# Experts' borders packed into two integers, and the result copy moved to the end of its pass

## What is computed

```python
h_shared = _swiglu(flat @ shared_in_w.T)
out_shared = h_shared @ shared_out_w.T + shared_out_b
...
e_probs = jax.nn.softmax(e_sel, axis=-1)
topv, topi = jax.lax.top_k(e_probs, K)
...
h_expert = _swiglu(flat @ expert_in_w.T)
...
for e in range(E):
    routed = routed + comb[:, e:e + 1] * (h_expert @ expert_out_weight[e].T)
return (out_shared + routed).reshape(Bx, Tx, Cx)
```

## Time and profile before

| what | value |
|---|---|
| median of 3 runs | 781.32 us (780.72 to 784.39) |
| profiled execution, its own time | 779.41 us |
| its span | 777.6 us |
| PE busy | 734.0 us (94%) |
| DVE busy | 409.9 us (53%) |
| ACT busy | 262.7 us (34%) |
| POOL busy | 168.0 us (22%) |
| PE's first instruction of the experts' loop part (L1611) | 563.5 us |
| last turning in the loop (L1611) | 711.7 us |

### The profile page before, as it was taken

One profiled execution on the slowest core, in us unless ns is written; L12 is line 12 of the kernel. 1 busy time (PEld: TensorE's weight loads), 2 busy tenths in 40 slices (PEclk: granted clock), 3 DMA queues, 4 the chain that ended last, 5 costly groups with the idle time before them and its releaser, 6 DMA issues.

```text
span 777.6 us, 11923 instructions
## 1 busy us (share of the span) xinstructions
PE 734.0 (94%) x4217; PEld 456.4 (59%) x4217; DVE 409.9 (53%) x809; ACT 262.7 (34%) x387; POOL 168.0 (22%) x167
## 2 busy tenths in 40 slices
PE   4998999998799999999999999999889999999998
PEld 4664777775457755656575654445745555555554
DVE  4877987795457766696435442222146434421154
ACT  2761222222255223236534213333345524422000
POOL 3320000000006000002222224444612222211462
PEclk9999999999999999999999999999969999999999
DMA  9200002000004114001234320111367866333674
GB/s 239 91 1 0 1 2 79 31 1 1 13 2 135 55 62 156 1 0 27 54 98 145 107 54 17 46 48 55 109 211 247 324 234 231 122 122 125 191 206 133
DMA packets 24368, 73.37 MB, mean 94 GB/s; under 512 B 7138, under 2 KB 7484, under 8 KB 20225
## 3 DMA queue, kind: packets, MB, share of 16 engines
q1 hardware_dynamic: 8607, 39.74, 15.3%
q0 software_dynamic: 10624, 24.99, 11.1%
q10 hardware_dynamic: 5090, 8.01, 2.8%
HBM read 57.38 MB, written 15.31 MB: 93 GB/s over the span
## 4 chain that ended last, share of the span: by engine, by line
PE 77%; DVE 9%; ACT 7%; DMA 3%; issue 2%; ACTq 1%; POOL 0%; DVEq 0%; POOLq 0%
PE banks L1272 58%; PE banks L1314 6%; PE banks L1302 6%; PE banks L1611 2%; DMA y_rows<-xT 1%; ACT W L411 1%; PE banks L1327 1%; DMA big<-in_proj_mat 1%; DVE st L733 1%; PE banks L1295 1%; DVE W L710 1%; PE banks L1482 1%; DVE xn L1092 1%; ACT big L579 1%; ACTq L457 1%
## 5 line engine op out<-in xcount | busy, mean ns | idle before, releaser
L1272 PE MATMUL banks<-W,xT 128*125 128x512 f16 (+1 forms) x1392 | 319.9, 384 | 8.0 <-ACT xT L677 1.9
L1272 PEld LDWEIGHTS banks<-W,xT 128*125 128x125 f16 (+1 forms) x1392 | 166.0, 122 | 139.0 <-issue 17.6
L1272 PE MATMUL banks<-xT,W 128*128 128x500 f16 (+1 forms) x720 | 131.3, 344 | 1.8 <-DVE xn L1224 1.4
L1272 PEld LDWEIGHTS banks<-xT,W 128*128 128x128 f16 x720 | 70.7, 98 | 60.4 <-issue 4.4
L710 DVE SCALAR_TENSOR_TENSOR W<-stg,W 128x2048 f16<-128x2048 f32 x30 | 68.8, 2313 | 42.7 <-ACT W L411 42.7
L1272 PE MATMUL banks<-W,big 128*125 128x512 f16 x360 | 81.5, 380 | 0.0
L1242 DVE CAST xT<-banks 128x1024 f32 x23 | 28.1, 1222 | 73.4 <-PE banks L1611 73.4
L1272 PEld LDWEIGHTS banks<-W,big 128*125 128x125 f16 x360 | 48.3, 136 | 29.2 <-issue 2.3
L353 POOL DMA_INDIRECT xn<-h_rows,tokidx x28 | 35.1, 1253 | 125.8 <-PE banks L1611 119.6
L342 POOL TENSOR_TENSOR big<-xn,big 125x512 f16<-125x512 f32 x20 | 23.5, 1173 | 173.1 <-ACT big L594 173.1
L411 ACT ACTIVATE W<-stg 128x2048 f16<-128x2048 f32 x30 | 56.4, 1904 | 0.0
(11 more groups left out here) (292 smaller groups left out, 861.3 us busy)
## 6 DMA issues: line engine op xcount, KB each, us to landing
stg<-in_units SPq DMA_DIRECT2D x30, 1024.0 KB, 5.0
y_rows<-xT ACTq DMA_DIRECT2D x29, 256.0 KB
h_rows<-big POOLq DMA_DIRECT2D x10, 500.0 KB, 3.6
out_x<-x SPq DMA_DIRECT2D x10, 224.0 KB
stg<-in_wqkT SPq DMA_DIRECT2D x2, 1024.0 KB, 11.5
x<-in_x SPq DMA_DIRECT2D x2, 896.0 KB
x<-in_x SPq DMA_DIRECT2D x1, 448.0 KB
xn<-h_rows,tokidx POOLq DMA_INDIRECT x28, 5.2
```

The lines of the kernel that those rows point to most:

```text
L1272: ins = te.matmul(dst, lhs(sl, c), rhs(sr, c), start=(first and c == 0 and k == 0), stop=(last and c == n - 1 and k == 2))
```

## The change

1. The eight ends of the experts are packed four by four, to the base 28, into two integers. DVE computes them in three instructions (one addition, two multiply-adds) where it wrote nine integers in two. `etab` holds two integers.
2. Each engine loads two integers in place of eight (`borders`). Division and remainder on registers are put where a border is used: at the end of each pass and between the experts' loops.
3. ACT and DVE read them during the shared product, behind group 21 of 24. PE reads them where it did.
4. On ACT, `result(0)` stands right behind the first high copy, ahead of the units U_EXP + 4 and + 5; a pass is `high(i + 1)`, `result(i + 1)`, and `result(total)` behind the loop goes. With that the units behind an expert follow the result copy of its last pass.

```diff
+PACK = NT + 1
...
-        etab = sb("etab", [1, EXP + 1], I32)
+        etab = sb("etab", [1, 2], I32)
+        etabf = sb("etabf", [1, 6])
...
+        def borders(eng):
+
+            ends = []
+            for z in range(2):
+                four = eng.value_load(etab[0:1, z:z + 1], min_val=0, max_val=PACK ** 4 - 1)
+                for k in range(4):
+                    e = 4 * z + k
+                    ends.append(eng.snap((four // PACK ** k) % PACK, min_val=e + 1, max_val=NT - EXP + e + 1))
+            return ends
...
@@ ACT @@
                         unit(U_EXP + n // 4 - 1)
-
-
-            act.wait_ge(S["etab_rdy"], 1)
-            starts = [act.value_load(etab[0:1, e:e + 1], min_val=e, max_val=NT - EXP + e) for e in range(1, EXP + 1)]
-            ends, total = starts, starts[EXP - 1]
+                    if n == 21:
+                        act.wait_ge(S["etab_rdy"], 1)
+                        starts = borders(act)
+                        ends, total = starts, starts[EXP - 1]
...
             s.activation(hgT[:, 0, 0], turned[0], ACT.Copy).then_inc(S["hg_h"], 1)
+            result(0)
             unit(U_EXP + 4)
             unit(U_EXP + 5)
             for e in range(EXP):
                 with act.Fori(0 if e == 0 else starts[e - 1], ends[e]) as i:
-                    result(i)
                     high(i + 1)
+                    result(i + 1)
                 for u in late_units(e):
                     unit(u)
-            result(total)
...
@@ DVE, route @@
-                v.tensor_copy(etab[0:1, 0:EXP], nt8[0:1, 1, :])
-                v.tensor_tensor(etab[0:1, EXP:EXP + 1], nt8[0:1, 1, EXP - 1:EXP], nt8[0:1, 0, EXP - 1:EXP], ALU.add).then_inc(S["etab_rdy"], 1)
+                ends8 = seen[0:1, TILES, :]
+                link(v.tensor_tensor(ends8, nt8[0:1, 1, :], nt8[0:1, 0, :], ALU.add))
...
+                v.scalar_tensor_tensor(out=etab[:, :], in0=quads[:, :, 1], scalar=float(PACK * PACK), in1=quads[:, :, 0],
+                                       op0=ALU.mult, op1=ALU.add).then_inc(S["etab_rdy"], 1)
...
@@ DVE, shared product; the same at n == 21 @@
+                    if n == 21:
+                        dve.wait_ge(S["etab_rdy"], 1)
+                        starts = borders(dve)
...
@@ PE, ahead of the loop @@
-            starts = [pe.value_load(etab[0:1, e:e + 1], min_val=e, max_val=NT - EXP + e) for e in range(1, EXP + 1)]
+            starts = borders(pe)
```

More of the change, by code:

```diff
@@ L1190, in route @@
                     link(v.tensor_tensor(nt8[:, 1, e:e + 1], nt8[:, 1, e - 1:e], nt8[:, 0, e - 1:e], ALU.add))
-                v.tensor_copy(etab[0:1, 0:EXP], nt8[0:1, 1, :])
-                v.tensor_tensor(etab[0:1, EXP:EXP + 1], nt8[0:1, 1, EXP - 1:EXP], nt8[0:1, 0, EXP - 1:EXP], ALU.add).then_inc(S["etab_rdy"], 1)
+                ends8 = seen[0:1, TILES, :]
+                link(v.tensor_tensor(ends8, nt8[0:1, 1, :], nt8[0:1, 0, :], ALU.add))
+                pairs = ends8.rearrange("p (z a b) -> p z a b", z=2, a=2)
+                link(v.scalar_tensor_tensor(out=etabf[:, 0:4].rearrange("p (z a) -> p z a", z=2), in0=pairs[:, :, :, 1], scalar=float(PACK), in1=pairs[:, :, :, 0],
+                                            op0=ALU.mult, op1=ALU.add))
+                quads = etabf[:, 0:4].rearrange("p (z a) -> p z a", z=2)
+                v.scalar_tensor_tensor(out=etab[:, :], in0=quads[:, :, 1], scalar=float(PACK * PACK), in1=quads[:, :, 0],
+                                       op0=ALU.mult, op1=ALU.add).then_inc(S["etab_rdy"], 1)
                 dve.wait_ge(S["etab_rdy"], 1)
@@ L1229, in _ @@
                         unit(U_EXP + n // 4 - 1)
-            dve.wait_ge(S["etab_rdy"], 1)
-            starts = [dve.value_load(etab[0:1, e:e + 1], min_val=e, max_val=NT - EXP + e) for e in range(1, EXP + 1)]
-            ends, total = starts, starts[EXP - 1]
+                    if n == 21:
+                        dve.wait_ge(S["etab_rdy"], 1)
+                        starts = borders(dve)
+                        ends, total = starts, starts[EXP - 1]
             dve.wait_ge(S["turned"], 1)
```

## The result

| | before | after |
|---|---|---|
| median | 782.86 us (780.72 to 784.67, 4 runs) | 813.13 us (809.85 to 814.99, 4 runs) |
| ratio, 95% interval | 1 | 1.0383 (1.033 to 1.0436) |
| profiled execution, its own time | 779.41 us | 814.99 us |
| its span | 777.6 us | 813.0 us |

The change makes the kernel 3.8% slower. The forecast was 808.0 us, range 795 to 817.

What follows compares the result with a forecast made beforehand. PE, busy 94% of the span, was taken as the bound. 779.41 - 3.0 (entry) + 20.4 (stalls) + 9.9 (clock) - 0.6 (given back) = 806.1 us, or 808.0 against the median; own range 802 to 813, wider 795 to 817.

Steps and rivals of the forecast that it cites:

- Rival (c): At the experts' borders: no stall, so only the entry's saving counts and the kernel is faster, 777.7 us; chance 0.07.
- The border of an expert: At six experts' ends, late weight units delay DVE's low copy, so PE stalls 3.4 us each, 20.4 us in all.
- The clock after each stall: Behind each of six border stalls PE's granted clock falls, costing 1.65 us each, 9.9 us in all.
- (a): At the six borders: the stalls come but the clock stays up, 798.1 us; chance 0.14.
- (b): Behind the six border stalls: the lower clock lasts twice as long per stall, 817.9 us; chance 0.07.
- The entry: Start of the experts' loop: fewer border loads and the first result copy ahead of the units save 3.0 us.
- L(1) doesn't spoil that: At the loop's entry: DVE's next low copy, behind the units, ends at 574.6, before the first product ends at 575.7.
- Rival (d): At the loop's entry: nothing is saved and the stalls stay, 811.0 us; its chance is inside the forecast's 0.70.
- The packing: DVE's three small instructions and unpacking on registers at pass ends: costed at nothing; other ends 0.4 and 1.2 us.
- Given back: In the loop: stalled passes leave time for waits on the previous result's DMA, returning 0.6 us, between 0 and 1.

Runs made afterwards that it cites:

- experiment 2: Two variants of the changed kernel with the low copy ahead of the units: DVE's loops shifted by one pass, 785.01 us; ACT's shifted too, 777.52 us.
- e1_pack_only: The changed kernel with ACT's old order put back, packed borders and early reads kept: 778.77 us, ratio 0.9984 to the kernel before.
- e2_order_only: The kernel before, with its eight border loads per engine, given only ACT's new order: 811.04 us, ratio 1.0397.
- e9_double_low: The changed kernel with DVE writing the low half of each of the twelve late units twice: 842.72 us, ratio 1.0776.
- e3_both_shifted: The changed kernel with ACT's and DVE's loops shifted by one pass, the second high and low copies ahead of the entry's units: 777.52 us, ratio 0.9962.
- e11_shifted_again: The same file as e3_both_shifted, run again beside the kernel before: 780.09 us, ratio 0.9987.

## Why the prediction was right, and where it was off

**Direction and mechanism: right.** The six idles ahead of a turning, ended by DVE's low copy, came as forecast. Rival (c), no stall, holds only for kernels that move L (experiment 2) or leave ACT's order (e1_pack_only).

**"The border of an expert", 6 x 3.4 = 20.4 us: 19.6 measured.** The chain held step by step. The units follow R by 1.40 us (587.93 - 586.53) where 1.36 was taken from the earlier trace rows. DVE's pair is 1.94 us behind, keeps it 4.41 us, and PE starts 0.44 us after the copy, where 0.42 was taken. The Trainium skill (Advanced Engine Details and Errata, Control Flow Timing) would have added about 0.1 us for the loop's end between R and the units. In the trace of the kernel after the compare-and-branch itself takes 40 to 50 ns on ACT (L699). The spacing of 1.40 us leaves room for 0.04 us, and the stalls came out shorter than 3.4 us rather than longer, so here the measurement speaks for less.

**"The clock after each stall", 9.9 us: 7.8 measured. This term was somewhat too large, and it left something out.** It priced a loss of clock of 1.65 us per border and took it for all that a stall costs behind its idle time; the turning behind a stall was put at its 1.06 us without a reason. Measured behind each stall are, on average, 1.30 us of clock and 1.16 us of slower turning, 14.8 us in all. The turning's part is not the clock. Stretches behind the first border, kernel after, and the turning behind the third:

```profile
594.00:597.50 3.50, 1.56 (x13) 1.20 (x13) 1.50 (x2) 0.00 (x0) 0.00 (x0) 1.00 0.96 351
598.00:601.00 3.00, 3.00 (x9) 1.05 (x9) 1.23 (x1) 1.02 (x1) 0.95 (x1) 0.50 0.84 303
601.00:604.00 3.00, 3.00 (x15) 1.42 (x14) 0.00 (x0) 0.00 (x0) 0.00 (x0) 0.98 0.32 126
...
632.26:634.46 2.20, 2.19 (x16) 1.67 (x17) 0.00 (x0) 0.00 (x0) 0.00 (x0) 0.50 1.00 398
```

The turning from 595.94 runs at 1.00 up to 597.5 at least and takes 2.17 us. Then the clock is at 0.50, its 1.2 GHz level, in M, and back near 2.4 GHz in the stretch from 601. The third turning runs at 0.50 throughout and takes 2.31 us, hardly more. The missed evidence was in the earlier trace rows: at 0.50 T(1), at 567.35, took 2.22 us behind a wait and T(0), whose addresses are constants, 1.87. T(1) took 2.20 to 2.23 us at the entry of every kernel. The prediction carried this 2.22 us over to the new entry and did not ask what it means for the turnings behind the stalls.

**Rivals (a) and (b): both fell, (b) at five borders of six.** The clock does fall, behind all six stalls (6.15 to 7.42 us for M). At the third border it was at 0.50 from 632.26 to 638.00 us, through the whole turning and most of M, which is some twice as long as at the others, and M lost 2.07 us; the mean of the six is below the forecast's 1.65. That it is paid at each wait anew agrees with the rule drawn on (the Trainium skill, TensorE: Matmul & The Clock Gate, HAM oscillation). The rows add how often: it was paid behind all eighteen border waits of 3.2 to 7.9 us (after, e2_order_only and e9_double_low), behind five of six of 1.8 us, behind three of six of 1.1 to 1.2 us, and behind none of six of 0.2 us.

**"The entry", -3.0 us: -3.3 measured, from other parts, so the close agreement is partly luck.** T(0) waits 2.08 us in place of 3.23, for POOL's announcement, as forecast: 1.15 us. M(0) no longer waits for R(0) and starts 2.98 us sooner, where 2.48 was forecast. M(0) took 5.91 us where 7.2 was expected, a larger gain from the clock. "L(1) doesn't spoil that" was wrong: L(1) ended at 578.49, only 0.08 us before M(0). T(2) had to wait 0.31 us and took 2.22 us instead of 1.06, by the same slow turning, which gave 1.5 us back. That the loads, and not T(0), held H(0) and L(0) was a reading on 0.07 us (565.41 + 0.23 against 565.71) and changes nothing in the sum. Rival (d) is out.

**"The packing", nothing: right.** DVE's three instructions took 0.15 us each and hid; e1_pack_only shows no loss from the divisions and remainders between passes. The loads, now two per queue, left the shared product alone: ACT still paused 1.28 us at each pass there.

**"Given back", 0.6 us: about 0.4 measured.**

**The sum.** Against the profiled execution 26.7 us were expected. The loop and entry made 30.7. The errors are -0.8 for the idles, -2.1 for the clock, +7.0 for the turnings, -0.3 at the entry and +0.2 for what is given back, together +4.0. The clock term, 2.1 too high, hid part of the 7.0 that was left out; that much of the agreement is luck. The median of 813.13 us lies in the range of 795 to 817, just past the upper end of the forecast's own 802 to 813. The profiled span grew by another 4.6 us, which belongs to the clock of that execution in unchanged code. The forecast stood on the median of 781.32 us, where the four runs now give 782.86, so against 26.7 us the medians moved by 30.3.

## What to carry to other kernels

When a copy that waits for a product is moved within an in-order queue, look at what stands behind it at the border of the loop as well as inside it: here weight conversions stood there, and another engine's copy behind them, so moving one instruction by one place shifted the chain by a whole product (5.35 us) against 2.0 us of slack. Price a stall of PE by its idle time plus what follows it, here the clock of the next product and a slower turning, whose register work had no time to run ahead; 3.3 us of idle cost 5.7. A change with two parts should be measured in two parts: one half of this one was harmless, and the loss was wholly in the other.

## What the runs showed of the hardware that was not expected

- A turning of 16 products of 128x128 with register addresses took 2.1 to 2.3 us when PE's queue had just waited, be it 0.17 us with a granted clock of 1.00 behind it or 7.9 us with one of 0.50, and 1.06 us when the queue had run ahead under a long product. The register instruction per product is 46 ns, but the distance between products grew from about 66 to about 130 ns, more than that; what the rest of it is was not looked into.
- M's loss to the clock did not grow with the wait before it: where it came, it was 1.4 us on average at 1.8 us of idle, 1.3 at 3.3 and 1.3 at 7.9. At 7.9 us the clock fell inside the wait (a mean of 0.58 from 597.0 to 600.4 at the first border), and the turning at 0.50 took no longer than one at 1.00. What changed was how often the loss came. Behind idles of 1.1 to 1.2 us it came three times in six, and no row shows why behind one and not the other.
- Two profiled executions of one kernel (e3_both_shifted and e11_shifted_again) differed by 5.3 us at the end of the last shared product, 558.49 and 563.79 us, and those of before and after by 4.6 us; in both pairs the granted clock from 189 to 197 us is 0.79 in the slower one and 1.00 in the other. A difference of some 0.5% between two single profiles needs the granted clock beside it before it is explained.
